# Routing one batch earlier, and a shorter way to the first keys: a linear-attention and mixture-of-experts kernel on one core

## The reference

```
q, k, v = split(x @ W_qkv)                 # 16 heads of 64
q, k = relu(q @ W_f + b_f), relu(k @ W_f + b_f)
kv = einsum('bhnd,bhne->bhde', k, v)
out = einsum('bhnd,bhde->bhne', q, kv) / (q . sum_n k + 1e-6)
x = layernorm(x + out @ W_out + b_out)
logits = x @ gate_w.T ; probs = softmax(logits) ; top 2 of 8 experts
y = gelu(x @ w1[e] + b1[e]) @ w2[e] + b2[e]      # F = 512, for both experts
x = layernorm(x + sum_k prob_k * y_k)
```

## Time and profile before

| | us |
|---|---|
| median of 3 runs | 466.5 (465.53 to 467.39) |
| profiled execution | 467.53 |
| its span, first to last instruction | 465.7 |
| PE busy | 435.6 (94%) |
| DVE busy | 302.6 (65%) |
| ACT busy | 272.3 (58%) |
| POOL busy | 162.2 (35%) |

### The profile page before, as it was taken

The page is one execution under the profiler, slowest core; times in us unless marked ns, Lnnn a source line. Parts: engine busy times, 40 slices in busy tenths (PEclk is TensorE's granted clock), DMA queues, the critical chain, the costliest instruction groups (busy, mean ns, idle before and its releaser), DMA issues.

```text
span 465.7 us, 8129 instructions
## 1 busy us (share of the span) xinstructions
PE 435.6 (94%) x2608; PEld 344.6 (74%) x2608; DVE 302.6 (65%) x899; ACT 272.3 (58%) x530; POOL 162.2 (35%) x164
## 2 busy tenths in 40 slices
PE   3999999999999999999999998999999999999940
PEld 2777776776776776776676675599999999999930
DVE  3383866986986976975975999665643222245784
ACT  2555656666665665665665663377555555555672
POOL 2101101112422421421421433067776555555550
PEclk9999999999999999999999999999999999999995
DMA  8920000000000000000000000788886987799343
GB/s 221 334 82 0 3 0 1 0 7 17 26 13 12 23 14 13 23 14 12 25 18 7 23 20 30 257 246 247 256 273 223 309 242 228 241 354 301 124 130 113
DMA packets 34442, 52.19 MB, mean 112 GB/s; under 512 B 4943, under 2 KB 24788, under 8 KB 34272
## 3 DMA queue, kind: packets, MB, share of 16 engines
q1 hardware_dynamic: 25136, 40.72, 28.5%
q0 software_dynamic: 4544, 8.54, 5.2%
q10 hardware_dynamic: 4720, 2.42, 1.8%
HBM read 39.82 MB, written 12.75 MB: 113 GB/s over the span
## 4 chain that ended last, share of the span: by engine, by line
PE 89%; DVE 4%; DMA 3%; issue 1%; ACT 1%; ACTq 1%; POOL 0%; POOLq 0%; SPq 0%; DVEq 0%
PE psA L640 14%; PE psO L532 12%; PE psG L649 9%; PE psA L434 6%; PE psA L436 6%; PE psA L435 6%; PE psS L649 6%; PE psA L511 6%; PE psG L523 3%; PE psG L554 3%; PE psG L434 3%; PE psG L435 3%; PE psA L579 3%; PE psG L436 3%; DMA bf_col<-bf 2%; PE psS L470 1%
## 5 line engine op out<-in xcount | busy, mean ns | idle before, releaser
L390 POOL DMA_INDIRECT expert_rows<-rows,pos x64 | 62.4, 976 | 114.2 <-DVE pos L1023 92.5
L415 POOL DMA_INDIRECT expert_results<-q_act,kT x56 | 55.2, 986 | 37.2 <-DVE q_act L1140 25.2
L668 ACT ACTIVATE kT<-psA,bf_col 128x512 f32<-128x512 f32 x64 | 43.9, 686 | 37.5 <-PE psA L436 37.2
L532 PE MATMUL psO<-qn,mixed 128*128 128x512 f32 x128 | 65.5, 598 | 0.0
L668 ACT ACTIVATE q_act<-psA,bf_col 128x512 f32<-128x512 f32 x64 | 43.9, 689 | 26.2 <-PE psA L436 26.1
L1054 DVE TENSOR_TENSOR qn<-q_act,psG 128x512 f32<-128x512 f32 x64 | 42.7, 680 | 5.3 <-PE psG L523 5.3
L819 DVE TENSOR_TENSOR k_lo<-psA,k_hi 128x512 fp32r<-128x512 f32 x64 | 43.5, 683 | 3.2 <-ACT k_hi L668 2.6
L511 PEld LDWEIGHTS psA<-cst,kT 128*128 128x128 f32 x256 | 31.1, 141 | 14.6 <-ACT kT L668 7.2
L434 PE MATMUL psA<-xT_hi,wk_hi 128*128 128x512 f32 x64 | 41.7, 652 | 0.0
L793 ACT ACTIVATE q_act<-psA,xT_raw 128x256 f32<-128x256 f32 x84 | 34.5, 470 | 10.7 <-PE psA L640 10.1
L511 PE MATMUL psA<-cst,kT 128*128 128x128 f32 x256 | 38.6, 273 | 1.5 <-DVE k_lo L819 1.5
(11 more groups left out here) (180 smaller groups left out, 903.1 us busy)
## 6 DMA issues: line engine op xcount, KB each, us to landing
xT_raw<-w SPq DMA_DIRECT2D x21, 578.0 KB, 4.6
x_raw<-w SPq DMA_DIRECT2D x18, 578.0 KB, 4.8
kT<-expert_rows SPq DMA_DIRECT2D x28, 132.0 KB, 4.0
x<-expert_results SPq DMA_DIRECT2D x4, 512.0 KB, 6.3
xT_raw<-xT SPq DMA_DIRECT2D x1, 1792.0 KB, 10.7
q_act<-wqkvT SPq DMA_DIRECT2D x3, 512.0 KB, 7.5
rn<-expert_rows SPq DMA_DIRECT2D x11, 132.0 KB
expert_rows<-zeros SPq DMA_DIRECT2D x9, 132.0 KB, 15.7
```

Source lines behind the costliest of these rows:

```text
L390: pool.indirect_dma_start(xs, bass.IndirectOffsetOnAxis(ap=pos_2[o % 2][:, j, k:k + 1], axis=0), rows_2[o % 2][:, j, k, :], None).then_inc ...
L415: pool.indirect_dma_start(ys, bass.IndirectOffsetOnAxis(ap=xrow[r][:, c, D:D + 1].bitcast(I32), axis=0), yrow[u][:, c, :], None, bounds_ch ...
L532: mm(psO[:, :], mixed[:, c, :], qn[:, c % 4, :], start=c == 0, stop=c == CH - 1).then_inc(o_pe, 1)
L668: return act.activation(out_, in_, func, **kw)
```

## The change

In the first stage: ten matmuls of zeros stand ahead of everything on PE. ACT issues the bias column ahead of the constants, and the constants in two transfers, the identity first. Keys begin as soon as the first half of the folded key weights is split; the query fold, the mean of the gate weights, and their splits go between the keys of batch 0. In the rounds: batch p = b-1 is routed in round b, its pick and mark behind the scaled logits, weigh and place behind the reciprocals, its ranks between two pieces of the gram matrix, ACT's exponents and fill around the gram copies. The early table moves from the second stage of round 7 into its key phase, with a buffer of its own (`past`). POOL scatters all eight pieces of batch b-2 in round b. SP waits for r_hl of batch 7 ahead of the first expert loads.

```diff
-        past = [qn_space[0:1, a * 704:(a + 1) * 704] for a in range(2)]
+        past = [sb(f"past{i}", [1, LATE * len(ERAS) * E]) for i in range(2)]
...
             sp.wait_ge(table, 2)
+            sp.wait_ge(r_l, B)
...
-                if 3 <= b < B:
-                    scatter(b - 3, range(TILES, PIECES))
                 if b >= 2:
                     scatter(b - 2, range(TILES))
-                if b == B - 1:
-                    pool.wait_ge(g_pe, 2 * b + 1)
+                    if b < B:
+                        pool.wait_ge(q_pe, CH * b + 1)
+                    else:
+                        pool.wait_ge(o_pe, CH * (b - 1) + 4)
                     scatter(b - 2, range(TILES, PIECES))
...
+            pe.wait_ge(zero_ready, 1)
+            for _ in range(10):
+                mm(psS[:, 0:P], zeros[:, 0, 0:P], zeros[:, 0, 0:P], start=True, stop=True)
...
-            pe.wait_ge(in_c, 16)
-            pe.wait_ge(in_small, 64)
-            mm(psS[:, 0:E], con("ones"), gw[:, :], start=True, stop=True).then_inc(mean_pe, 1)
-            pe.wait_ge(in_fold_q, 16)
...
+                    if b == 0 and c == 2:
+                        fold_queries()
+                    if b == 0 and c == 3:
+                        gate_mean()
...
-                if old:
-                    ranks(o)
...
                     norms()
                     gram(0, (2, 3))
+                    if prev:
+                        ranks(p)
...
-            act.dma_start(cst[:, :], consts[:, 0:_C["spread"][0]]).then_inc(in_c, 16)
+            for r in (0, DH):
+                act.dma_start(bf_col[r:r + DH, :], bf.rearrange("(d a) -> d a", a=1)).then_inc(in_bf, 16)
+            act.dma_start(cst[:, 0:P], consts[:, 0:P]).then_inc(in_ident, 16)
+            act.dma_start(cst[:, P:], consts[:, P:_C["spread"][0]]).then_inc(in_c, 16)
...
+                    if b == 0 and c == 4:
+                        act.wait_ge(fold_pe, 3)
+                        hi(wq_hi[:, :], psG[:, :, :].rearrange("p a s -> p (a s)")).then_inc(fold_hi, 1)
+                    if b == 0 and c == 5:
+                        tokens_hi()
...
-                    if old and c == 1:
-                        router.pick()
-                    if old and c == 2:
-                        router.mark()
-                    if old and c == 5:
-                        router.weigh()
+                    if b == B - 1 and 1 <= c <= 5:
+                        early_table(c - 1)
...
-                if b == B - 1:
-                    for part in range(3):
-                        early_table(part)
                 if cur and prev:
                     means(p)
                     scale_logits(p)
+                    router.pick()
+                    router.mark()
...
-                    if b == B - 1:
-                        early_table(3)
-                        early_table(4)
+                    if prev:
+                        router.weigh()
+                        router.place()
```

More of the change, by code:

```diff
@@ L443, in _, with fold_queries, gate_mean @@
                     last.then_inc(fold_pe, 1)
-            pe.wait_ge(in_c, 16)
-            pe.wait_ge(in_small, 64)
-            mm(psS[:, 0:E], con("ones"), gw[:, :], start=True, stop=True).then_inc(mean_pe, 1)
-            pe.wait_ge(in_fold_q, 16)
-            for c in range(CH):
-                last = mm(psG[:, c // 4, c % 4 * P:(c % 4 + 1) * P], wqkvT_sb[:, c, :], wfd[:, :], start=True, stop=True)
-            last.then_inc(fold_pe, 1)
+            def fold_queries():
+                pe.wait_ge(in_fold_q, 16)
+                for c in range(CH):
+                    last = mm(psG[:, c // 4, c % 4 * P:(c % 4 + 1) * P], wqkvT_sb[:, c, :], wfd[:, :], start=True, stop=True)
+                last.then_inc(fold_pe, 1)
+            def gate_mean():
+                pe.wait_ge(in_c, 16)
+                pe.wait_ge(in_small, 32)
+                mm(psS[:, 0:E], con("ones"), gw[:, :], start=True, stop=True).then_inc(mean_pe, 1)
             def fold_values():
@@ L502, in turn_keys @@
                         pe.wait_ge(m_first, b)
+                    if c == 0 and b == 0:
+                        pe.wait_ge(in_ident, 16)
                     if c == 1 and prev:
@@ L736, in attention @@
                     hi(x_hi[:, :, :], x_raw[:, b * TILES:(b + 1) * TILES, :]).then_inc(x_h, 1)
+                if cur:
+                    key(0)
+                    if b:
+                        tokens_hi()
                 for c in range(CH):
@@ L761, in attention @@
                         hi(gm[:, h * 512:(h + 1) * 512], psG[:, h, :]).then_inc(g_done, 1)
+                        if h == 0 and prev:
+                            fill(p)
                     act.wait_ge(n_step, N_STEPS * (b + 1))
@@ L845, in _ @@
             dve.wait_ge(cleared_row, 6)
+            for i in range(2):
+                dve.wait_ge(fold_hi, i + 1)
+                at_ = slice(i * 512, (i + 1) * 512)
+                lo(wk_lo[:, at_], psA[:, 1, at_], wk_hi[:, at_]).then_inc(fold_lo, 1)
             dve.wait_ge(in_c, 16)
+            dve.wait_ge(in_ident, 16)
             dve.tensor_copy(ones_b[:, :], con("ones")).then_inc(cast, 1)
@@ L1079, in attention @@
                         column_sums(c // 2)
[L1080 to L1085 removed]
+                    if b == B - 1 and 1 <= c <= 5:
+                        early_table(c - 1)
+                    if b == 0 and c == 6:
+                        dve.wait_ge(mean_pe, 1)
+                        dve.wait_ge(in_small, 32)
+                        dve.scalar_tensor_tensor(gwc[:, :], psS[:, 0:E], -1.0 / D, gw[:, :], ALU.mult, ALU.add).then_inc(gwc_ready, 1)
+                        dve.wait_ge(fold_hi, 3)
+                        lo(wq_lo[:, :], psG[:, :, :].rearrange("p a s -> p (a s)"), wq_hi[:, :]).then_inc(fold_lo, 1)
                 if cur:
```

52 lines of the change are left out of this document (18 added, 34 removed).

## The result

The changed kernel takes **468.75 us** (median of 8 runs, 468.4 to 470.24), the kernel before on the same chip 466.62 (8 runs): ratio 1.0052, 95% interval 1.0036 to 1.0067. It is 2.1 us slower, where 3.5 us less were forecast. The profiled execution took 470.24 us with a span of 468.4 (before: 467.53, 465.7).

What follows compares the result with a forecast made beforehand. PE was taken to bound the kernel nearly everywhere, except the start, batch 7's end and the tail. -6.5 + 0.3 + 3.3 - 0.1 - 0.4 = -3.4, rounded to -3.5, gave 463.0 us; own range 461.5 to 465, whole range 459.8 to 465.9.

Steps and rivals of the forecast that it cites:

- the start: Start up to the last k_hi of batch 0: -6.5 us, bounds -7.3 and -4.5.
- the ordinary batches: Batches 2 to 6: moved routing fits VectorE's idle gaps with 0.5 us left, so cost 0.
- batch 7: Early table in the key phase of batch 7 makes PE wait: +3.3 us, from 2.5 to 3.6.
- (a): Start: bf_col, issued earlier on ACT's queue, lands at 8.9 us; the identity at 9.7 to 10 us.
- (b): Start: key fold at 6.23 us, PE warmed up, first kT at about 9.5 us instead of 17.76, 8.3 us earlier.
- (c): Inside batch 0: query fold and wq split between the keys give back 1.8 us, bounds 1.0 and 2.8.
- rival 2: Start gains half, from PE staying at 1.2 GHz or bf_col and identity landing late: 465.7 us, chance 0.16.
- +0.3: Batch 1: routing's small PE products are new there and cost 0.3 us.
- Rival 3: Second stage cannot hold the routing, rn or r_hl delayed: 469 us, decides from 0.5 us per batch, chance 0.06.
- Round 8: Pick, mark, weigh and ranks leave a phase in which PE waits for DVE: -0.4 us.
- SP's new wait: Before the first expert loads: loads go out at r_hl, about 2 us sooner than before, cost 0.
- -0.1: Batch 7 behind L554: the table no longer holds up r_hl, weigh and place fit in its place, -0.1 us.

Runs made afterwards that it cites:

- the repeat: The changed kernel itself, unaltered, run again in the second group beside the kernel before: 468.89 us, ratio 1.0041.
- the mended rounds: Changed kernel with the early table's parts spread over round 7 and xT_lo held until hot_sum is written: 476.68 us, ratio 0.984; later ratios 0.9837, 0.9783.

## Why the prediction was wrong

The forecast's sum failed at three terms: the start (-6.5, measured -3.2), the ordinary batches (0, measured +0.7) and batch 7 (+3.3, measured +5.0). In each of the three a mechanism was missing.

**(a), (b) the first kT, -8.3: measured -6.3.** The mechanism was right: warm-up, a faster key fold, an earlier first kT. The term that failed is "ACT's split follows xT_hi, 7.25 to 7.85". It took ScalarE's issues at their old length; they took 1.13 and 1.17 us here, xT_hi came at 8.42 instead of 6.57, and the first kT at 11.50. bf_col was priced well: 8.9 us forecast, landed at some 8.5 (2.9 + 5.6). The identity was not: "9.7 to 10 us" against 11.6 (3.53 + 8.1). With a first kT at 9.5 it would have been the next hold.

**(c) given back, +1.8: measured +3.0.** The query fold took 1.79 us and the wq split 1.03, as priced. What was left out stands behind the first kT: in the profiled execution the fallen clock, some 1.7 us; in the repeat, where the clock stayed, the constants that VectorE got at 15.4, with k_lo 1.9 us late (first kT to last k_hi 14.9 us there). Together the start gained 3.2 us, 3.1 in the run with it alone, and not 6.5. Both conditions of rival 2 came in part, late landing and lower clock; it had 0.16. The earlier trace rows warned: a small transfer took 7.68 us amid the weights.

**"+0.3" in batch 1: nothing.** The gap from batch 0 to batch 1 is 34.26 us, 34.24 before. The routing's products on TensorE stood ahead of the norms from round 2 on and now stand behind the norms from round 1 on. Either way the gap from batch 1 to batch 2 is the first to have them.

**"Cost 0" for the ordinary batches: wrong by 0.7 us.** The sum on VectorE was right to 0.1 us: in batch 3 rn begins 1.92 us after the start of the norms, as before. But it priced hot_sum from a place where GpSimd computes nothing. Moved, it meets xT_lo with 0.11 us to spare, and takes 1.2 us in the two batches in which pick has its gap of 0.17 to 0.32 us. That costs 1.0 us; 0.3 come back from lighter key phases. Rival 3's limit of 0.5 us was passed twice by a mechanism that it did not have.

**Batch 7, +3.3: the wait right, its consequence missed.** Where the clock is kept, the cost is 3.3 to 3.6 us; where it fell, 1.7 more. The prediction used the clock's fall for the start and not here.

**Round 8, the first expert block and SP's new wait:** -0.1 - 0.4 = -0.5 us was forecast, and from b7 to the first expert product it is -0.3 (20.02 after 20.34). The span's tail gave 0.5 back, so that +0.1 is left.

**The sum.** The start missed by 3.3 us, batch 1 by -0.3, the ordinary batches by 0.7, batch 7 by 1.7, what follows it by 0.6: 6.1 before rounding, on a forecast of -3.4 makes +2.7, the difference of the spans (+2.1 in the medians). No one of the misses would have made it slower; the rivals priced them one at a time, and rival 2 alone stops at 465.7.

**A reading of the prediction that can't be shown.** It says that TensorE ran at 1.2 GHz in the start of the kernel before. The durations say so (3.61 us against 1.78 for as many records of the same shape), but the granted clock of that trace reads 1.00 from 0 to 22 us. From 9 us on in the changed kernel, and in batch 7, the two agree.

What stays open: no run with the mended rounds fell on an occasion where the kernel before takes 467 us. Its norms of batch 7 come at 275.66, 277.82 and 276.25 in the three traces; with 185.4 behind them and 1.8 between span and time, an estimate from these rows is 463 to 465 us.

## What to carry to other kernels

Before an operation is moved on VectorE, look at what GpSimd does at the new place: if both read two tensors from SBUF, the price is the other's whole length, and a slack of 0.5 us must be held against 1.3, not against 0.19. An order that holds by 0.11 us does not hold: make it sure with a wait, which cost nothing here. A wait on TensorE of 2 us is priced twice, with and without what runs behind it at 1.2 GHz (1.7 us here, in five traces of seven); taking the wait away cured it, and filling it with zeros is not proven. And a start in which weights are loading is shortened by less than the work that is moved off its chain: list what lands next, for it can become the hold. Such a start varies from one execution to the next by more than a change in it is worth (b0 from 33.6 to 38.0 us), so one trace of it decides nothing; the medians do.

## What the runs showed of the hardware beyond this

- ScalarE's DMA issue of the gate weights took 0.44 us in the kernel before and, at its later place, 0.69 to 2.48 us in the traces with the changed start, and it holds the activations behind it. The second part of the constants took 0.44 to 0.80 us in most traces, 1.57 and 1.82 in two. Big loads were in flight in all of them; what makes one issue long was not taken apart.
- After a wait of some 2.06 us the granted clock fell to 1.2 GHz (0.50) for the outputs at 271 us in five of seven traces; in two, with the same wait, it stayed at 1.00. In the start it fell after waits of 2.02, 2.30, 2.37, 2.80 and 3.30 us, and did not after 2.50, 2.52 and 2.78.
- A key fold of 16 records took 2.05 to 2.5 us in most traces, but 3.78 in three of those with a warm-up, as in all three without, with the granted clock at 1.00 in all: how well the ten products prepare it depends on the execution, and the granted clock does not tell.
- The time behind batch 7's norms differs by the occasion: 185 against 196 to 206 us, with the gaps of attention equal (34.24 to 34.56 us in ordinary batches on either).
